# An adaLN block with attention and eight experts: another order for the sums and side steps of the expert pipeline

## The reference, cut to what matters

```
h   = layernorm(x) * (1 + cb) + sb                # per batch
hd  = h @ down_w + down_b                         # 256 -> 128
p   = softmax(h @ router_w + router_b - cost)     # 8 probabilities per row
top2, gates = top_k(p, 2), softmax of the two     # gates -> weights w_e per row
out = sum_e w_e * (gelu(gelu(hd) @ w1_e + b1_e) @ w2_e + b2_e)
out = out + 0.1 * (gelu(gelu(hd) @ sw1 + sb1) @ sw2 + sb2)
out = out @ up_w + up_b + gelu(h) @ core_w + core_b
x   = x + gb * out
```

## Time and profile before

| | us |
|---|---|
| median of 3 runs | 832.74 |
| lowest and highest run | 831.82, 833.17 |
| the profiled execution, whole time | 831.92 |
| its span, first to last instruction | 830.1 |
| busy PE, DVE, ACT, POOL over the span | 793.3, 686.1, 625.8, 440.5 |
| the stage of the experts, from 628 to the end: span | 203 |
| busy PE, DVE, ACT, POOL in it | 177.4, 158.3, 131.0, 108.9 |

### The profile page before, as it was taken

How to read it: one execution, slowest core, us unless ns; L and a number is a source line. 1 busy time by engine, 2 the same in 40 slices (tenths; PEclk the granted TensorE clock), 3 DMA queues, 4 the chain that set the end, 5 groups by cost and what they waited for, 6 DMA issues and landing times.

```text
span 830.1 us, 14458 instructions
## 1 busy us (share of the span) xinstructions
PE 793.3 (96%) x4806; PEld 706.1 (85%) x4806; DVE 686.1 (83%) x1655; ACT 625.8 (75%) x1409; POOL 440.5 (53%) x305
## 2 busy tenths in 40 slices
PE   7999899999999999999999999999999889999997
PEld 6789888999999999999999999999987767777676
DVE  4789988888888888888888888789998996787865
ACT  4787877887788878887788877887879566767772
POOL 2554465545445665445655654664444564757543
PEclk9999999999999999999999999999999998999998
DMA  7263223332333334222344323343222211212121
GB/s 262 63 176 78 65 70 100 101 90 64 85 76 89 90 99 110 67 64 65 74 110 115 91 65 80 82 132 90 65 64 65 76 65 43 72 35 91 36 95 39
DMA packets 47594, 70.55 MB, mean 85 GB/s; under 512 B 5536, under 2 KB 38464, under 8 KB 47392
## 3 DMA queue, kind: packets, MB, share of 16 engines
q1 hardware_dynamic: 47008, 68.81, 31.4%
q0 software_dynamic: 368, 0.81, 0.3%
q10 hardware_dynamic: 144, 0.00, 0.0%
HBM read 25.49 MB, written 2.17 MB: 33 GB/s over the span
## 4 chain that ended last, share of the span: by engine, by line
PE 62%; ACT 19%; DVE 11%; issue 5%; POOL 1%; DMA 1%; POOLq 0%; SPq 0%; DVEq 0%
PE M L723 10%; PE M L722 10%; PE M L721 9%; PE T L721 6%; PE T L723 6%; PE T L722 6%; PE S L721 5%; PE S L723 4%; PE S L722 4%; ACT PB L616 4%; ACT PB L662 3%; ACT pth L689 2%; DVE S L1121 2%; ACT qk L675 2%; ACT hh L655 1%
## 5 line engine op out<-in xcount | busy, mean ns | idle before, releaser
L616 ACT ACTIVATE PB<-S,nb 128x128 f32<-128x128 f32 (+3 forms) x256 | 133.9, 533 | 109.3 <-DVE nb L1121 109.3
L566 POOL TENSOR_TENSOR X<-X,fb 128x512 f32<-128x512 f32 x64 | 83.2, 1299 | 247.6 <-DVE fb L1158 247.6
L573 POOL TENSOR_TENSOR ptl<-ptl,pth 128x640 fp32r<-128x640 f32 x126 | 195.9, 1577 | 31.8 <-ACT pth L689 31.8
L662 ACT ACTIVATE PB<-PB,ri 128x256 f32<-128x256 f32 (+3 forms) x256 | 124.5, 581 | 6.4 <-DVE ri L1130 6.3
L1121 DVE CUSTOM_DVE_ANT_0 S<-S,cc 128x128 f32<-128x128 f32 (+3 forms) x256 | 117.5, 522 | 1.3 <-PE S L723 1.3
L1106 DVE TENSOR_TENSOR qk<-M,qk 128x512 fp32r<-128x512 f32 x108 | 74.6, 691 | 45.2 <-ACT qk L675 45.2
L1137 DVE STREAM_TRANSPOSE gab<-PB 128x256 f32<-128x256 f32 (+2 forms) x192 | 109.2, 621 | 0.0
L721 PE MATMUL S<-qk 128*128 128x128 f32 (+3 forms) x256 | 86.6, 338 | 4.7 <-DVE qk L1106 4.7
L721 PE MATMUL M<-hh,W 128*128 128x512 f32 x222 | 86.6, 390 | 1.5 <-DVE hl L1092 1.5
L689 ACT CAST pth<-ptl 128x640 fp32r<-128x640 f32 x128 | 87.9, 746 | 0.0
L723 PE MATMUL M<-hh,W 128*128 128x512 f32 x222 | 86.5, 390 | 0.0
(11 more groups left out here) (255 smaller groups left out, 2442.2 us busy)
## 6 DMA issues: line engine op xcount, KB each, us to landing
ptl<-gab SPq DMA_DIRECT2D x256, 160.0 KB, 3.1
stage<-in_wat SPq DMA_DIRECT2D x16, 512.0 KB, 4.9
gab<-scw SPq DMA_DIRECT2D x16, 256.0 KB, 3.1
tmp<-scw SPq DMA_DIRECT2D x16, 256.0 KB, 3.4
X<-in_x SPq DMA_DIRECT2D x3, 512.0 KB, 7.7
stage<-in_wfa SPq DMA_DIRECT2D x3, 512.0 KB, 4.6
out<-X SPq DMA_DIRECT2D x3, 512.0 KB, 2.6
X<-in_wmod SPq DMA_DIRECT2D x1, 1024.0 KB, 12.3
```

The costliest lines, as they stand in the source:

```text
L566: pool.tensor_tensor(X[:, a:a + 512], X[:, a:a + 512], fb[:, c2 * 512:c2 * 512 + 512], ALU.add).then_inc(s_y, 1)
L573: pool.tensor_tensor(ptl[u % 2][:, s], ptl[u % 2][:, s].bitcast(F32), pth[u % 2][:, s].bitcast(F32), ALU.subtract).then_inc(s_pl, 1)
L616: ins = act.activation(PB[:, P_OFF[i]:P_OFF[i] + w], PS[bk][:, a:a + w], ACT.Exp, bias=nb[:, i:i + 1], scale=-1.0, accum_out=sm[:, i:i + 1])
L662: act.activation(p, p, ACT.Copy, scale=ri[:, i:i + 1]).then_inc(s_P3, 1)
```

## The change

Three things change in the list, and one in the code of TensorE.

1. The loop now writes the `acc` of an expert ahead of the `w1` and `w2` of the same step. On VectorE the weighted product (L1234) stands ahead of the low part of the newest chunk, where it stood behind it and behind the side events of the step. It waits for the `w2` of that step, which stands behind `w1` on TensorE.
2. In batch 0, `wt` 0 with its three `wl` moves from chunk 7 to chunk 8, behind `z` 63, which it stood ahead of. The transposes `h2` 2 0 and `h2` 2 1 come one chunk later (the first now behind `dn` 1), `h2` 3 1 four later, behind `wt` 1, `r` 2 and `D` 1. `D` 0, `hs` 0 k, `gx` 0 k and `up` 0 k come some chunks later in batch 1. `o` 0 comes one later. The routers of batches 2 and 3, with `r` and `wt`, come one chunk later (the `wt` of batch 1 stays).
3. Batch 3's core product, 24 matmuls of 256 columns in `up` 3 0 and `up` 3 1, becomes an event `ug` of its own, ahead of `o` 3 and both `up` products.

The `wt`, `D` places of batches 2 and 3 now lie one chunk apart where they lay two apart (`D` does not move).

```diff
--- before.py
+++ after.py
@@ -124,25 +124,27 @@
     put(0, 4, ("rs", 0, 10), ("rs", 0, 11), ("rs", 0, 12))
     put(0, 5, ("rs", 0, 13), ("rs", 0, 14), ("pt", NU - 1))
     put(0, 6, ("wh", 22))
-    put(0, 7, ("wt", 0), ("wl", 0), ("wl", 1), ("wl", 2), ("z", NU - 1))
-    put(0, 8, ("st", 6, 0), ("st", 6, 1))
+    put(0, 7, ("z", NU - 1))
+    put(0, 8, ("wt", 0), ("wl", 0), ("wl", 1), ("wl", 2), ("st", 6, 0), ("st", 6, 1))
     put(0, 9, ("wo", last, 0), ("st", 6, 2), ("st", 6, 3))
     put(0, 10, ("wo", last, 1), ("wl", 3), ("nm", 6, 0))
     put(0, 11, ("nm", 6, 1), ("d0", 0))
-    put(0, 12, ("h2", 2, 0), ("d0", 1))
-    put(0, 13, ("dn", 1), ("d0", 2))
-    put(0, 14, ("h2", 2, 1))
+    put(0, 12, ("d0", 1))
+    put(0, 13, ("dn", 1), ("h2", 2, 0), ("d0", 2))
+    put(0, 15, ("h2", 2, 1))
     for k, j in enumerate((14, 15, 15, 16)):
         put(0, j, ("st", 7, k))
     put(0, 17, ("nm", 7, 0), ("dta", 0))
     put(0, 18, ("nm", 7, 1), ("dta", 1))
     put(0, 19, ("dta", 2), ("xb", 0))
     put(0, 20, ("h2", 3, 0))
-    put(1, 0, ("dt",), ("h2", 3, 1))
-    put(1, 2, ("hs", 0, 0))
-    put(1, 4, ("gx", 0, 0), ("hs", 0, 1))
-    put(1, 6, ("gx", 0, 1), ("D", 0))
-    for b, n in ((1, 5), (2, 22), (3, 43)):
+    put(1, 0, ("dt",))
+    put(1, 4, ("h2", 3, 1))
+    put(1, 5, ("D", 0))
+    put(1, 6, ("hs", 0, 0))
+    put(1, 8, ("gx", 0, 0), ("hs", 0, 1))
+    put(1, 10, ("gx", 0, 1))
+    for b, n in ((1, 5), (2, 23), (3, 44)):
         def at_(i, *events):
             put(*divmod(i, NC + 1), *events)
         at_(n, ("r", b))
@@ -154,34 +156,35 @@
             at_(n + m, ("rs", b, k))
         at_(n + (21 if b > 1 else 17), ("wt", b))
     for t in range(1, B):
+        late = 3 * (t == 1)
         put(t, 3, ("D", t))
-        put(t, 6, ("o", t - 1))
-        put(t, 8, ("up", t - 1, 0))
-        put(t, 9, ("hs", t, 0))
-        put(t, 10, ("up", t - 1, 1))
-        put(t, 11, ("gx", t, 0), ("hs", t, 1))
-        put(t, 13, ("gx", t, 1))
+        put(t, 6 + late // 3, ("o", t - 1))
+        put(t, 8 + late, ("up", t - 1, 0))
+        put(t, 9 + late, ("hs", t, 0))
+        put(t, 10 + late, ("up", t - 1, 1))
+        put(t, 11 + late, ("gx", t, 0), ("hs", t, 1))
+        put(t, 13 + late, ("gx", t, 1))
         if t + 1 < B:
             put(t, 17, ("dn", t + 1))
             put(t, 19, ("xb", t))
     put(B - 1, 18, ("xb", B - 1))
     chunks = B * (NC + 1)
     plan, later = [], []
-    for n in range(chunks + LAG):
-        if n < chunks:
-            plan.append(("w1", n))
-        if n >= LAG:
-            plan.append(("w2", n - LAG))
-        plan += at.get(divmod(n, NC + 1), [])
+    for n in range(chunks + LAG + 1):
         m = n - LAG
-        if m >= 0 and EXP_OF(m) != EXP_OF(m + 1) and EXP_OF(m) != (0, 1) or m == FIRST_ACC:
+        if 0 <= m < chunks and EXP_OF(m) != EXP_OF(m + 1) and EXP_OF(m) != (0, 1) or m == FIRST_ACC:
             t, e = EXP_OF(m) if m != FIRST_ACC else (0, 1)
             plan.append(("acc", t, e))
             if e and 8 * t + e + 3 < 8 * B:
                 later.append(8 * t + e + 3)
         while later and ("wt", later[0] // 8) in plan and ("wl", 3) in plan:
             plan.append(("wl", later.pop(0)))
-    plan += [("o", B - 1), ("up", B - 1, 0), ("up", B - 1, 1)]
+        if n < chunks:
+            plan.append(("w1", n))
+        if LAG <= n < chunks + LAG:
+            plan.append(("w2", m))
+        plan += at.get(divmod(n, NC + 1), [])
+    plan += [("ug", B - 1, 0), ("ug", B - 1, 1), ("o", B - 1), ("up", B - 1, 0), ("up", B - 1, 1)]
     return plan
 
 
@@ -907,16 +910,26 @@
                     pe.wait_ge(me, use[("wt", t)] + 1)
                     pe.wait_ge(me, use[("dt",)] + 1)
                     pe.matmul(o[:], Dm[:], wT(t), start=True, stop=True).then_inc(mf, 1)
+                elif kind == "ug":
+                    _, t, c2 = ev
+                    o = bank(("up", t, c2))
+                    pe.wait_ge(me, use[used_before[("up", t, c2)]] + 1)
+                    pe.wait_ge(s_xl, 2 * t + 2)
+                    for c in range(2):
+                        cx = 2 * c2 + c
+                        for k in range(2):
+                            mm3(o[:, 256 * c:256 * c + 256], lane(gx_at(t, k), 128 * cx, 128),
+                                wt(0, F_CORE + 256 * k, 256), c == 0 and k == 0, False)
                 elif kind == "up":
                     _, t, c2 = ev
                     pe.wait_ge(s_xl, 2 * t + 2)
                     for c in range(2):
                         cx = 2 * c2 + c
                         oo = o[:, 256 * c:256 * c + 256]
-                        for k in range(2):
+                        for k in range(2 if t < B - 1 else 0):
                             mm3(oo, lane(gx_at(t, k), 128 * cx, 128), wt(0, F_CORE + 256 * k, 256), k == 0, False)
                         pe.wait_ge(s_oc, t + 1 + (c2 if t == B - 1 else 0))
-                        ins = mm3(oo, lane((oh, ol), 128 * cx, 128), wt(0, F_UP, 256), False, True)
+                        ins = mm3(oo, lane((oh, ol), 128 * cx, 128), wt(0, F_UP, 256), False, c == 1 or t < B - 1)
                     ins.then_inc(mf, 1)
```

## The result

| | before | after | forecast |
|---|---|---|---|
| median, us | 832.65 | 824.04 | 817.3 (811.5 to 823.0) |
| lowest and highest run | 831.82, 833.17 | 823.45, 824.61 | |
| span of the profiled execution | 830.1 | 822.2 | |
| ratio, 95% interval | | 0.9897 (0.988 to 0.9915) | |

The changed kernel is faster by 8.6 us. I had forecast 15.4, and the time lies 1.0 us above my range. Lines of `after` are 3 higher than before in the code of GpSimd, ScalarE and most of TensorE, and 13 higher in VectorE's.

What follows compares the result with a forecast made beforehand. TensorE was taken to set the pace in later batches, VectorE in batch 0. Gains of 5.8 us (through `up` 0 1), 6.5 (rest of batches 1 to 3) and 3.1 (tail), 15.4 together, gave 817.3 us, range 811.5 to 823.

Steps and rivals of the forecast that it cites:

- Batch 0 up to `r` 2: Up to the end of `r` 2: VectorE ends batch 1's router 3.9 us earlier, `r` 2 ends at 691.3.
- The term for the meetings: Batch 0: VectorE's small steps stand still beside GpSimd's work; fewer such meetings were taken as a gain of 1.0 us.
- The wait before `up` 0 0: Batch 1: TensorE stands still 3.3 us for the core input, 16.8 us from `r` 2's end to `up` 0 0.
- The clock behind it: Behind the new wait before `up` 0 0: a low clock was taken to cost 1.0 us.
- Batches 1 to 3: Rest of batches 1 to 3: product and router waits go, `D` 3 gets worse; 6.5 us gained (bounds 4 and 7.5).
- The product waits: Batches 1 to 3: TensorE's seven waits for VectorE's weighted product go, 5.0 us.
- the 2.2 at `wt` 2 and 3: Routers of batches 2 and 3: TensorE's waits of 2.4 us shrink to 0.2 as GpSimd's `X` add ends earlier.
- the rival "meetings": VectorE's steps meet GpSimd elsewhere, `wt` 2 and 3 wait as before, 2.4 us more: 819.7; chance 0.12.
- The tail: After the last `w2`: core-product matmuls cover the last sum; 3.1 us gained (bounds 2.4 and 3.3).
- The reading of the bound: Batch 0: VectorE sets the pace, so closing TensorE's gaps wins nothing unless VectorE gets on too.
- The expectation that the clock shows no loss in batch 0: Batch 0: a sign of being right was no work lost to a low clock there.
- the sign that the product waits fall under 1.5 us: TensorE's waits for VectorE's weighted product, all batches: they fall from 7.3 to under 1.5 us.

Runs made afterwards that it cites:

- e4: The changed kernel with GpSimd's sums and bias addition of batch 0 on 8 columns, the rest of batch 0's sum left out; 818.92 us.
- e1: The kernel before with only the new loop, weighted sums ahead of the next up product; 819.68 us.
- e9: The changed kernel with the later core inputs and the routers of batches 2 and 3 put back to their old places; 820.98 us.
- e11: The changed kernel with only the later core inputs put back, routers left where the change has them; 823.53 us.
- e17: The changed kernel with GpSimd's bias addition as four instructions of 128x256 instead of one of 128x1024; 824.47 us.
- e3: The kernel before with only the moved places, old loop and old tail; 831.17 us.
- e7: The changed kernel with GpSimd's bias addition of batches 1 and 2 moved behind the second chunk of the next batch; 828.12 us.
- e14: The changed kernel with batch 0's sums of chunks 10, 11, 17 and 18 held back at the chunk's end; 826.86 us.

## Why the prediction was wrong

**Batch 0 up to `r` 2: the step that failed.** I had reckoned VectorE 3.9 us earlier, 3.6 of idle time less 0.7 and plus 1.0 for fewer meetings. The idle time did go, from 3.6 to 1.4 us:

```profile
DVE prod L1247 <- DMA gab<-scw: 0.8, 1, 0.8
DVE hl L1105 <- ACT M L659: 0.6, 1, 0.6
```

The 0.8 is the wait for the weights that I had put at 0.7. The term for the meetings was wrong in sign and size. It stood in the sum as a gain of 1.0, and it was a loss of 4.2: the normalization took 5.2 us more, and the other steps together took 1.0 less, 0.7 of it one `rs<-mv` of 128x4 that had stood beside a sum before (0.88 us, now 0.16). The router of batch 1 ended at 693.25 instead of 687.4:

```profile
693.06 0.19 DVE L1013 TENSOR_TENSOR wgw<-wg,wgw 128x32 fp32r<-128x32 f32 x1
```

From the first `z` that is 1.3 us later than before, where I had it 3.9 earlier. e4, with the additions thin, has it 3.5 earlier. The rest of the reckoning held: the idle time and the earlier end of batch 0's router gave 3.0 us for my 2.9, and from here to the end of `r` 2 it took 3.8, as forecast. I had seen such a step and priced one meeting more or less at up to 1.8, but took it for chance. It was not: an order that puts the product ahead starts GpSimd's sum beside whatever VectorE does next, and the list shows that in three chunks of batch 0 (10, 11 and 17) this is a normalization, with its operands in SBUF; the fourth step meets the bias addition. `r` 2 ended at 697.07, where I had 691.3. Of these 5.8 us, 5.2 are this term (a loss of 4.2 for a gain of 1.0) and 0.7 the attention, which ended later in this execution (633.25 for 632.58), a part that nothing in the change touches.

**The wait before `up` 0 0** came as reckoned: 3.1 for 3.3 us, and from the end of `r` 2 to its start 16.7 for 16.8:

```profile
713.78 0.35 PE L724 MATMUL M<-W,gxh 128*128 128x256 f32 x1 [3.12 <-DVE gxl L1285]
```

The clock behind it lost 1.7 where I took 1.0. For both parts I had 5.8 us; at a `w1` behind `up` 0 1 with the same work done (724.58 before, 723.89 after) the gain is 0.7. The miss of 5.1 is the 5.2 above. e4 got it back: 5.3 us at this `w1`, counted from the first `z`.

**Batches 1 to 3**: 4.1 us for 6.5. The product waits gave 4.5 of 5.0, `D` 3 waits 1.1 as forecast. The failed term is the 2.2 at `wt` 2 and 3, where 0.1 came. The reason that I gave holds for the sums alone (e1: 0.2 and less), and I did not ask what the routers' place, one chunk later, does to it. There the last router steps stand behind one more product, whose sum runs beside them. e9, with the routers back, waits 0.2 at each, e11, without that, 0.7 and 1.1, so the place decides it; how much of the wait is meetings is not separated, since e17, with the addition in pieces, waits as long. This is the rival "meetings", priced there with these 2.4 us only. I had the mechanism and this place, and left out the larger place, the normalization of batch 0, at a chance of 0.12.

**The tail** was right: 3.2 us less from the start of the last `w2` to the end of the span, for 3.1. From the last `w2` to the end of the last VectorE step it is 6.5 us, where 6.4 was forecast:

```profile
813.24 0.28 PE L724 MATMUL M<-W,gxh 128*128 128x256 f32 x1
...
813.44 0.42 DVE L1259 TENSOR_TENSOR prod<-T,gab 128x256 f32<-128x256 f32 x1 [1.47 <-PE T L726]
...
819.01 0.69 DVE L1311 TENSOR_TENSOR X<-X,fb 128x512 f32<-128x512 f32 x1
```

0.7, 4.1 and 3.2 us make up the difference of the spans, 7.9, within rounding. The median's gain is 0.7 more, since the execution profiled before lay 0.7 below its median.

**The reading of the bound** was half right. VectorE did set the pace in batch 0. But the conclusion that the moved places let VectorE get on was not: alone they gave 1.6 us (batch 1's router ended 1.1 us earlier from the first `z` in e3), and beside the sums they took 3 to 5 away. The expectation that the clock shows no loss in batch 0 was wrong too: 1.7 us behind the wait of 2.9. So was the sign that the product waits fall under 1.5 us: they are 4.8, of which batch 0 has 4.3.

## What to carry to other kernels

When an instruction on one engine starts work on GpSimd, look at which VectorE instructions come in the following microsecond and where their operands lie. Here small steps and normalizations with all operands in SBUF were held until GpSimd's addition of 256 to 1024 columns ended; steps that read PSUM were not, and a power of 8 columns held no normalization. Make one edit of a bundle at a time: here one of three parts gave more than the whole. And where an engine has no slack, a wait removed at one place comes back at the next, so count a saved wait only after naming what is late next. And when the executions of one kernel differ by more than the edit is worth, compare stretches of the traces, from an event that the edit does not touch.

## What the runs showed of the hardware

A held VectorE step ends within 0.05 us of GpSimd's instruction in the three small router steps shown (734.42 and 737.44 of the change, 737.70 of e7), and GpSimd's instruction keeps its own length: sums of 128x512 take 1.28 or 1.29 us, the bias addition 2.36 to 2.41, beside a held step. With two GpSimd instructions in a row, each of a pair of VectorE instructions is held by one of them (2.79 us for both in place of 0.73). The recorded start of the held pair, 664.34, lies 0.1 us ahead of GpSimd's, 664.44, so the recorded starts do not tell who will be held. What is held here are scalings and casts with one operand in SBUF, as well as additions and products with two. The Trainium skill, page "SBUF — State Buffer", section "Who interferes with whom", says that casts and scalings in a two-port mode, and instructions with two inputs in SBUF, share ports with GpSimd, and that a blocked one waits for the whole instruction. The rows agree as far as they go: a `CAST` took 2.22 us, a `TENSOR_SCALAR` 1.29 and a `TENSOR_TENSOR` with two inputs in SBUF 0.90, and the PSUM readers stayed at 0.68. In which mode a cast or a scaling ran, no row shows.

The clock takes a part that I could not predict. In e7, waits of 2.7 and 2.1 us are each followed by a stretch of 20 us at 0.83; in the changed kernel one of 3.1 us costs 1.7 us and one of 2.0 us, at 686.5, costs nothing, while in e9 one of 2.0 us there has 1.7 us lost behind it. The same program ran at mean clocks from 0.979 to 0.989 (e14), in times up to 8 us apart. What decides between these is not settled by the runs here.
